# A memset of 128 instead of 256 columns between GpSimd's scatters (a four-layer graph network on one Trainium2 core)

## The reference, cut to what matters

```python
edge_index = jnp.stack([src, dst])
h = jnp.maximum(_layernorm(x, axis=-1), 0.0)
x = x + _L0_gnn_ref(h, L0_gnn_W1, L0_gnn_W2, L0_gnn_b, src, dst)
h = jnp.maximum(_layernorm(x, axis=-1), 0.0)
x = x + _L1_gnn_ref(h, edge_index, edge_weight, L1_gnn_W, L1_gnn_b, ...)
...   # layer 2 (edges without weights, batch norm) and layer 3 (attention over the edges)
```

## Time and profile before

| | |
|---|---|
| median of 3 runs | 2204.69 us |
| the profiled execution's own time | 2204.25 us |
| its span in the profile | 2202.4 us |
| up to 486 us | clearing, `dedupe`, degrees; scatters of columns 0 to 303 |
| 486 to 1315 us | the main loop over 25 tiles; scatters of columns 304 to 805, until 1240 us |
| 1315 to 2202 us | the rest of layer 1, layers 2 and 3 |

### The profile page before, as it was taken

How to read it: one execution, slowest core, us unless ns; L and a number is a source line. 1 busy time by engine, 2 the same in 40 slices (tenths; PEclk the granted TensorE clock), 3 DMA queues, 4 the chain that set the end, 5 groups by cost and what they waited for, 6 DMA issues and landing times. The chain is left out here.

```text
span 2202.4 us, 23568 instructions
## 1 busy us (share of the span) xinstructions
PE 1871.7 (85%) x7253; PEld 1153.6 (52%) x7253; DVE 1331.8 (60%) x1958; ACT 484.9 (22%) x635; POOL 1023.4 (46%) x1346
## 2 busy tenths in 40 slices
PE   5599768779999999755566699999879999999996
PEld 1178622257777777433345457777753444434442
DVE  6877678844444445422222355565458788878885
ACT  1000200025555555322233334200250000000000
POOL 1688777777888888888888400000005000000000
PEclk9755579889999999977778899999699999999998
DMA  7888860016666677433343441587016555656553
GB/s 269 328 328 328 336 226 9 9 61 240 239 239 239 243 243 254 157 120 120 140 159 131 167 142 63 192 283 242 27 42 171 155 158 167 189 163 179 166 164 102
DMA packets 338855, 395.86 MB, mean 180 GB/s; under 512 B 114026, under 2 KB 319572, under 8 KB 325843
## 3 DMA queue, kind: packets, MB, share of 16 engines
q1 hardware_dynamic: 219872, 307.83, 39.9%
q10 hardware_dynamic: 93110, 86.22, 11.9%
q0 software_dynamic: 25792, 0.87, 1.0%
HBM read 222.33 MB, written 172.51 MB: 179 GB/s over the span
## 5 line engine op out<-in xcount | busy, mean ns | idle before, releaser
L373 POOL DMA_INDIRECT table<-valT,idxT x806 | 815.9, 1012 | 251.5 <-issue 249.9
L1994 PE MATMUL psum<-wgt,big 128*65 128x384 f32 (+3 forms) x1600 | 527.7, 491 | 2.7 <-POOL big L1855 2.7
L1944 DVE SCALAR_TENSOR_TENSOR wgt<-ratio,l3q,fcj 128x768 f32<-128x768 f32 (+2 forms) x400 | 414.1, 1053 | 96.6 <-PE psum L1994 83.5
L1994 PEld LDWEIGHTS psum<-wgt,big 128*65 128x65 f32 x1600 | 219.0, 137 | 302.5 <-issue 296.0
L784 PE MATMUL psum<-hx,region 128*128 128x257 f32 x1250 | 299.2, 387 | 5.5 <-DVEq L572 5.0
L784 PE MATMUL psum<-region,g 128*128 128x512 f32 (+1 forms) x672 | 270.1, 547 | 1.0 <-DVE big L587 1.0
L587 DVE TENSOR_TENSOR big<-big,psum 128x512 f32<-128x512 f32 (+1 forms) x325 | 209.6, 664 | 86.8 <-PE psum L784 86.4
L784 PEld LDWEIGHTS psum<-hx,region 128*128 128x128 f32 x1250 | 233.6, 195 | 36.5 <-DVEq L572 5.4
L852 PE MATMUL psum<-ident,tk 128*128 128x128 f32 x625 | 104.8, 304 | 151.2 <-DMA tk<-table 150.7
L991 POOL PARTITION_ALL_REDUCE edges<-edge x1 | 0.5, 516 | 396.7 <-DVEq L1363 396.7
L784 PEld LDWEIGHTS psum<-region,g 128*128 128x128 f32 x672 | 121.9, 190 | 118.9 <-issue 112.8
(11 more groups left out here) (215 smaller groups left out, 1487.9 us busy)
## 6 DMA issues: line engine op xcount, KB each, us to landing
table<-tk SPq DMA_DIRECT2D x25, 3200.0 KB
fcj<-counts SPq DMA_DIRECT2D x150, 384.0 KB, 3.3
tk<-table SPq DMA_DIRECT2D x25, 1664.0 KB
counts<-region ACTq DMA_DIRECT2D x25, 1600.0 KB
tk<-table SPq DMA_DIRECT2D x25, 1536.0 KB
fcj<-counts SPq DMA_DIRECT2D x50, 448.0 KB, 3.6
counts_t<-region ACTq DMA_DIRECT2D x25, 800.0 KB
counts_b<-region ACTq DMA_DIRECT2D x25, 800.0 KB
```

The lines of the kernel that those rows point to most:

```text
L373: eng.indirect_dma_start(out=table, out_offset=bass.IndirectOffsetOnAxis(idxT[:, c:c + 1], 0), in_=valT[:, c, :], in_offset=None, bounds_c ...
L1944: eng.scalar_tensor_tensor(out=wgt[:, n % NW, u, 0:w], in0=rb[:, 2 * i + u, t0 * P:t0 * P + w], scalar=qs[:, k, 2 * i + u:2 * i + u + 1], ...
L1994: last = eng.matmul(acc[p % 2][u][0:FW, b, 0:hi - lo], ftx[:, k, 2 * i + u, :], wgt[:, n % NW, u, lo:hi], start=k == 0, stop=k == NT - 1, ...
```

## The change

`rest` becomes half as wide, and so does the memset that fills it. The number of memsets, their places, waits and semaphores stay, and so does every instruction of the other engines.

```diff
@@ -252,7 +252,7 @@
         od2 = buf("od2", [P, 2, NT])
         od3 = buf("od3", [P, 2, NT])
         g1 = buf("g1", [P, D])
-        rest = buf("rest", [P, 2 * P])
+        rest = buf("rest", [P, P])
         st1, mv1 = buf("st1", [P, 6]), buf("mv1", [P, 2])
         ln1 = buf("ln1", [P, 4])
         pF, pB, pW = psum[:, 0, :], psum[:, 1, :], psum[:, 2, :]
```

## The result

The changed kernel takes 2149.2 us, the median of four runs (2145.7 to 2157.78), against 2203.86 us for the kernel before beside it, now with a fourth run. The ratio is 0.9761, 95% interval 0.9747 to 0.9774. The forecast was 2150.6 us. The profiled execution took 2150.07 us and has a span of 2148.1 us, 54.3 us less than before; its own time fell by 54.2.

What follows compares the result with a forecast made beforehand. GpSimd's queue was taken to set the loop's end, with TensorE the bound up to 886 us. 502 memsets x 0.107 = 53.7 us off 2204.25 gave 2150.6 us; range 2137 to 2162, for 8 in 10 2137 to 2167.

Steps and rivals of the forecast that it cites:

- The two regimes: Main loop: TensorE's pace first, 26.8 us a tile; later GpSimd's, 47.1 us a tile, until the last scatter.
- A column's price: GpSimd's memset in the loop: 0.833 ns a column, so 128 fewer columns save 0.107 us each time.
- The 65 us of the bare spans: Alternative sum for the 502 memsets, from durations 0.34 less 0.21 us; the prediction used 54 us by starts.
- One for one: A shorter memset brings the next scatter forward by the full 0.107 us; spacing goes from 1.46 to about 1.36 us.
- the hidden 0.14 us: Part of the 0.30 us idle between bare scatters that runs beside the memset; 0.23 us of memset still covers it.
- The savings beside a full TensorE: GpSimd's savings while TensorE is the bound aren't lost: 264 memsets by the load at 883.9, 28 us sooner.
- the recurring stops: Five GpSimd stops, 112 scatters apart, 2.06 to 7.20 us idle; all stay, putting about -7 to +9 us around the forecast.
- Rival 1: In the loop, the memset's width doesn't set the scatter spacing; 2204 us, chance 4%.
- Rival 2: In the loop, the memset is covered below some width and spacing falls to the bare 1.28 us; 2114 us, chance 3%.
- Rivals 3 and 4: The first: denser scatters compete with tile loads and stores, giving back part; 2170 us, chance 7%. Rival 4: own line.
- Rival 4: Scatters in the busy stretch pass into the slow form of 160 to 240 us; 2228 us, chance 3%.
- signs of being wrong: Spacing staying above 1.40 us, recurring stops growing past 7 us, or the last scatter moving without the end following.

Runs made afterwards that it cites:

- the early half alone: Against the kernel before, memsets of 128 columns up to edge column 565 and 256 after it: 2176.28 us, ratio 0.9862.
- the first six experiments: No memset; one column; 512 bf16 columns; narrow only early; narrow only late; memset ahead of all 806 scatters: 2103.34, 2109.43, 2306.33, 2176.28, 2181.38, 2170.72 us.

## Why the prediction was right, point by point

**The bound.** Right. The two regimes were read from SyncE's waits and the load times, and the border moved as worked out: loads at 877 and 921 us were forecast, 879.0 and 918.9 came. The busy share of GpSimd over the span, 46%, would have missed it.

**A column's price.** 0.107 us for 128 columns; 105 ns by the memset's median, 108 ns by the spacing (1.464 to 1.356). The loop's 24 ns above the isolated row stayed with the place: 232 ns in the loop against the 0.21 us of the earlier trace rows, as it was 337 against 0.31. The 65 us of the bare spans would have come from taking one row in the loop and one outside; the two spans of the loop itself, 337 and 232 ns, give 105 ns and 53 us. The run with bf16 adds that the price is by column.

**One for one.** Right in this range, and the reason given for it too: the hidden 0.14 us are a floor that one column reaches and 128 don't.

**The savings beside a full TensorE.** They aren't lost; the early half alone gave 29.0 of the 52.2 us.

**The sum.** 53.7 us were forecast, 54.2 came in the profiled execution. Part by part in it: the spacing 502 x 0.108 = 54.2; the recurring stops 1.2 less (18 us above the median spacing, before 19); the start of the loop 1.0 sooner; and 2.0 us given back behind the last scatter (965.35 us from its start to the end of the span, before 963.32). These small ones lie inside the 7 to 9 us that the stops were granted. Across the first six experiments that tail is 961.8 to 966.1 us, so 2 us say nothing. That the total came out within 1 us is partly luck: the prediction itself left 7 to 9 us for the stops.

**The rivals.** Rival 1 (the width doesn't set the spacing) fell with the change itself (1.464 to 1.356 us) and with the run with 512 columns, and holds only below the floor. Rival 2 (the spacing falls to 1.28) is true of a narrower memset, not of this one. Rivals 3 and 4 would have shown in the kernel without memsets, and didn't. Rival 4 was also priced too high: its 79.4 us for 49 scatters hold one of the recurring stops, 5.9 us above the usual spacing, which the earlier trace rows don't show. Without it they are 1.53 us apart and not 1.65, and 264 scatters of that kind would have made 2196 us instead of 2228. Its argument that DMA is nearly as busy in the loop is loose as well: the share is 0.69 there against 0.82 from 160 to 240 us.

**The stops.** Right that they come by count: all five kept their columns (they follow the scatters of columns 336, 448, 560, 672 and 784 in the changed kernel, and in every variant that issues all 806). But one of the prediction's signs of being wrong was met to the letter: a stop past 7 us. The first is 7.5 us now. It was 7.2 before, so the sign was badly drawn; what counts is the sum, and that fell from 19 to 18 us:

```profile
537.91 0.97 POOL L373 DMA_INDIRECT table<-valT,idxT  x1 [7.53 <-issue]
```

**Late tiles.** TensorE's wait that ends at 1103.4 us was 18.63 us long before; in the changed kernel the one that ends at 1100.8 us is 15.02, 3.6 less where 3.3 were expected.

## What to carry to other kernels

An engine that is idle half the span can still own the end: look at what the late loads wait for, and then count all of its queue back to its first instruction, since time gained while another engine is the bound is kept as a head start. Cost an instruction by the spacing that it makes, from start to start, with and without it; the part that hides beside its neighbour is a floor for what removing it can give. And try the spacer at nothing before choosing its size: here no memset at all is 46 us faster than the changed kernel.

## What the runs showed of the hardware

- GpSimd's memset costs 0.82 to 0.84 ns a column in f32 and in bf16 alike (128 ns at 1 column, 232 at 128, 337 at 256, 553 at 512 of bf16).
- Between two indirect DMAs of 128 cells on GpSimd lie 1.277 us from start to start, 0.30 of them idle; a memset of one column fits in without moving them.
- GpSimd stops at every 112th of these scatters, for some 1.4 to 8 us above its usual spacing. In the kernels that issue all 806 it keeps its places by count, whatever the spacing. In the one that left out 120 there was none behind the 672nd that it issued, close to one of its waits for landings. What the stop waits for wasn't tried.
- All slow scatters lie beside a VectorE operation. In none of the nine profiles does a scatter without one beside it take over 1.0 us (246 of them in the kernel before, at most 0.99). There, 30 scatters beside the bf16 operation of 3328 columns take 1.60 to 2.66 us, and those beside the ones of 650 columns mostly 1.15. With a memset ahead of every scatter the two kinds have medians of 1.45 and 1.07 us. Other VectorE operations have a few slow scatters beside them as well. No run took the VectorE operations away, and no row shows by which mode or port they would slow a scatter, so the cause is not shown.
